# The last batch's gated expert product: weighing, transposed copies, output product and store divided over engines and halves

## The chip, the cores and the metric

The kernel runs on one core of a Trainium2 chip (trn2). The metric is the device time of one execution in microseconds (us), as the median of several runs.

## The reference, cut to what matters

A text stream `x` of 4 batches of 512 tokens by 128 channels goes through four residual blocks: a cross attention with a state-space filter, a butterfly feed-forward, a second cross attention, and a mixture of 8 experts of rank 32, of which each token takes the best two. Only the last block is touched:

```python
logits = jnp.einsum('bnd,de->bne', x, gate_w)      # x: after a layer norm
topv, topi = jax.lax.top_k(logits, 2)
w = jax.nn.softmax(topv, axis=-1)
u = jnp.einsum('bnd,edr->bner', x, Wu)
v = jnp.einsum('bnd,edr->bner', x, Wv)
s = jax.nn.silu(u) * v
Y = jnp.einsum('bner,erd->bned', s, Wo)
y_sel = jnp.take_along_axis(Y, topi[..., None], axis=2)
out = jnp.einsum('bnkd,bnk->bnd', y_sel, w)
# and around it
x = x + jnp.tanh(g_ffn[1]) * out
```

The kernel forms `s` for all 8 experts (8 times 32 = 256 columns), weighs it by the gate (zero for the experts that were not chosen), and multiplies by the 256 by 128 matrix `Wo`, which is the same sum.

## The kernel before, in words

Each batch's 512 tokens lie as four tiles (t = 0 to 3) of 128 tokens, one token per partition. The work is cut into steps with a name and a batch, such as `moe_out/3`; one table, `ORDER`, writes out by hand the order of the steps on each of the four compute engines: TensorE (PE), ScalarE (ACT), VectorE (DVE) and GpSimd (POOL). An engine takes its steps strictly in that order; a step waits on semaphores for what other engines have to have done. A second table, `BANKS`, gives the PSUM bank of each product; a product that reuses a bank first waits for the readers of the bank's former content. The four batches run interleaved, so while one batch waits on one engine the other engines have steps of other batches. Batch 3 is the last, and at its end there is nothing left to interleave.

The last block of one batch b is made of these steps:

- `top2` on DVE (with one exponential on ACT) makes the gate weights `W8`, 8 numbers for each token (L1305 to L1334).
- `units0` to `units3`: PE multiplies a token tile by `Wu` and `Wv`, 512 columns into one bank; ACT writes the silu of the first 256 columns to SBUF as tile t of `SUT` (L1000 to L1005); DVE multiplies it by the other 256 columns and counts up the semaphore `gated` (L1335 to L1338).
- `gate0` and `gate1` on POOL: each weighs two tiles of `SUT` (512 elements in each partition) by `W8`, and counts up `weighted` (L1573 to L1578).
- `turn0` and `turn1`: PE waits for both gate steps, and for each half j of the 256 columns transposes the four token tiles into a bank (L679 to L684, the transposes on L683). ACT copies each bank into `SU` (L1006 to L1010, through its helper on L837).
- `moe_out`: PE waits for both copies and makes the output product, 4 tiles by 2 halves j, 8 matmuls that the trace shows as 16 records (L685 to L692, through the helper on L499). DVE then adds the whole bank to `X` (L1339 to L1341, through the helper on L1118).
- SyncE (SP) waits for that addition and issues one store of the batch (L480 to L482), 256 KB, with 1 KB for each partition and half c of the tokens. At the very end it waits until all four stores have landed (L483).

The ends of the engines' orders before the change are: PE `units3/3 moe_out/2 turn0/3 turn1/3 moe_out/3`; ACT `units3/3 turn0/3 turn1/3`; DVE `units3/3 moe_out/2 moe_out/3`; POOL `gate0/3 gate1/3`.

In the trace, `SUT` lies in the buffer shown as `pack_bfly`, `SU` in `arena`, `W8` in `bt`, and all PSUM banks are shown as `bank`. POOL's element-wise helper is on L1496, ACT's on L837.

Of the kernel before, what the change touches and what calls it, by code (L numbers as in the profile page):

```python
# [7 lines left out]
B, S, D = 4, 512, 128  # L8
P = 128
NT = S // P  # L10
# [26 lines left out]
def columns(parts):  # L37
    at, out = 0, {}
    for name, n in parts:
# [46 lines left out]
        units1/1 units2/1 units3/1 lift4/3 wo/2 q/3 lift5/2 turn0/1 scoreA0/3 turn1/1 scoreA1/3 units0/2  # L86
        scoreA2/3 units1/2 scoreA3/3 units2/2 units3/2 maxT/3 keyA0/3 logits/2 keyA1/3 mixA0/3 keyA2/3 normA/3
        mixA1/3 mixA2/3 moe_out/1 wo/3 turn0/2 lift5/3 turn1/2 logits/3 units0/3 units1/3 units2/3 units3/3
        moe_out/2 turn0/3 turn1/3 moe_out/3
    """,  # L90
    "act": """
        s_kgen0 s_plag s_masks s_m0 s_qlag s_trig s_psin0 s_qsin rs0/0 score0/0 s_vw s_pexp winv0/0 score1/0
# [11 lines left out]
        rs3/3 rs5/1 keyA2/2 lift3/3 fold_up0/3 fold_up1/3 top2/1 rs4/3 normA/2 units0/1 units1/1 units2/1  # L104
        units3/1 lift4/3 q/3 lift5/2 turn0/1 rs5/2 turn1/1 units0/2 units1/2 units2/2 units3/2 maxT/3 keyA0/3
        keyA1/3 keyA2/3 top2/2 normA/3 turn0/2 lift5/3 turn1/2 rs5/3 top2/3 units0/3 units1/3 units2/3
        units3/3 turn0/3 turn1/3
    """,
    "dve": """
        s_kgen0 s_wq s_k0 s_consts s_coef s_parg0 s_parg1 s_qarg stat0/0 round0_0/0 round1_0/0 round2_0/0  # L110
# [17 lines left out]
        wo/1 norm2/3 stat5/1 x1/3 moe_out/0 stat3/3 norm3/3 top2/1 fold_down/3 stat4/3 normA/2 units0/1  # L128
        units1/1 units2/1 units3/1 wo/2 stat5/2 scoreA0/3 scoreA1/3 scoreA2/3 scoreA3/3 maxT/3 units0/2
        units1/2 units2/2 units3/2 top2/2 normA/3 wo/3 stat5/3 moe_out/1 top2/3 units0/3 units1/3 units2/3  # L130
        units3/3 moe_out/2 moe_out/3
    """,
    "pool": """
        s_row s_coef pick0/0 s_qal s_film pick1/0 s_ufly0 s_rows weigh0/0 s_ufly1 s_dfly0 s_dfly1 pick2/0
# [3 lines left out]
        gain/0 x1/0 mixi/1 s_v1 film_pre/1 k1/0 weigh1/2 weigh2/2 pick3/2 pick0/3 k1/1 weigh3/2 x_bias/1  # L138
        pick1/3 gain/1 x1/1 mixi/2 weigh0/3 mixr/2 film_pre/2 k1/2 weigh1/3 pick2/3 pick3/3 weigh2/3 weigh3/3
        x_bias/2 x_bias/3 gain/2 film_pre/3 mixi/3 gate0/0 gate1/0 gain/3 norm4/3 k1/3 gate0/1 gate1/1 gate0/2  # L140
        gate1/2 gate0/3 gate1/3
    """,
}

# [27 lines left out]
    "logits": [("logits", "logits")],  # L172
    **{f"units{t}": [(f"uv{t}", f"units{t}")] for t in range(NT)},
    **{f"turn{j}": [(f"turn{j}", f"turn{j}")] for j in range(2)},
    "moe_out": [("moe", "moe_out")],
    "s_k0": [("k0", "s_k0")], "s_m0": [(f"m0_{i}", "s_m0") for i in range(B)],
    "s_vw": [("wvf", "s_vw")], "vw": [("vw", "vw")],
    "s_w1": [("w1c", "s_w1")], "s_moe": [("moec", "s_moe"), ("goc", "s_moe")], "s_cw1": [("w1x", "s_cw1")], "s_cwup": [("wupx", "s_cwup")],
# [10 lines left out]
    for step, _, b, banks in ((*word.partition(":")[0].partition("/"), word.partition(":")[2]) for word in """  # L189
# [17 lines left out]
        scoreA1/3:4765 units0/2:1 scoreA2/3:7046 units1/2:2 scoreA3/3:0754 units2/2:0 units3/2:5 maxT/3:6  # L207
        keyA0/3:4607 logits/2:3 keyA1/3:4536 mixA0/3:72 keyA2/3:5140 moe_out/1:1 wo/3:0 turn0/2:7 lift5/3:6
        turn1/2:0 logits/3:4 units0/3:1 units1/3:6 units2/3:7 units3/3:5 moe_out/2:0 turn0/3:6 turn1/3:1
        moe_out/3:5  # L210
    """.split())
}

# [18 lines left out]
def build(nc, dram, out_dram):  # L232
# [5 lines left out]
    with ctx:  # L238
# [158 lines left out]
        def readers(name, b):  # L397
            if name.startswith("lift"):
                return [(lifted[int(name[4:])], b + 1)]
            if name.startswith("turn"):  # L400
                return [(s["turned"], 2 * b + int(name[4:]) + 1)]
            if name.startswith("uv"):
                return [(s["gated"], NT * b + int(name[2:]) + 1)]
            if name.startswith("score"):
                g = NT * b + int(name[5:])
                return [(s["first_round"], 2 * H0 * (g + 1)), (s["exps_done"], g + 1)]
            if name.startswith("sA"):
                g = NT * b + int(name[2])
                return [(s["maxed"], RG * g + int(name[4]) + 1)]
            if name.startswith("kA"):  # L410
                return [(s["probs_ready"], RG * (NCH * b + int(name[2])) + int(name[4]) + 1)]
            if name.startswith("up"):
                return [(s["up_gelu"], HT * b + int(name[2]) + 1)]
            if name.startswith("fup"):
                return [(s["fup_gelu"], HT * b + int(name[3]) + 1)]
            if name.startswith("kern"):
                return [(s["kern_copied"], int(name[4:]) + 1), (s["kern_moved"], int(name[4:]) + 1)]
            if name.startswith("m0_"):
                return [(s["m0_copied"], int(name[3:]) + 1)]
            if name.startswith("t1_"):  # L420
                return [(s["t1_copied"], 2)]
            return {
                "attnT": [(s["attnT_copied"], b + 1)], "fa": [(s["filmed"], b + 1)], "fb": [(s["filmed"], b + 1)],
                "down": [(x_ready["v"], b + 1)], "d0": [(s["dft_moved"], b + 1)],
                "d1": [(s["dft_copied"], 2 * b + 2)], "y": [(s["y_scaled"], b + 1)],
                "fc": [(s["ao_ready"], 2 * b + 1)], "fd": [(s["ao_ready"], 2 * b + 2)],
                "fdown": [(x_ready["x2"], b + 1)], "q": [(s["q_copied"], b + 1)],
                "mT": [(s["maxT_copied"], b + 1)], "pv": [(s["out_ready"], b + 1)], "sums": [(s["out_ready"], b + 1)],
                "wo": [(x_ready["x3"], b + 1)],
                "logits": [(s["logits_copied"], b + 1)],  # L430
                "moe": [(s["x4_ready"], b + 1)], "k0": [(s["k0_masked"], B)],
                "wvf": [(s["wvf_copied"], 1)], "moec": [(s["moe_centered"], 1)], "goc": [(s["moe_centered"], 3)], "w1x": [(s["w1_centered"], 1)], "wupx": [(s["wup_copied"], 2)], "vw": [(s["vw_copied"], b + 1)],
                "w1c": [(s["b1_done"], 1)], "fr0": [(s["freq_copied"], 2)], "fr1": [(s["freq_copied"], 3)],
                "wup": [(s["wup_copied"], 1)], "bup": [(s["bup_done"], 1)], "t2": [(s["t2_copied"], 1)],
                "wdn": [(s["wdn_copied"], 1)], "k1": [(s["k1_copied"], b + 1)],
                "v1a": [(s["v1_masked"], B - 1)], "v1b": [(s["v1_masked"], B)],
            }[name]
# [19 lines left out]
        def _(sp):  # L457
# [19 lines left out]
                sp.dma_start(by_parity(X[:, b, :, :]), tokens(dram["x"][b])).then_inc(x_loaded[b], 16)  # L477
            for name in ("rows", "att1", "moe"):
                sp.dma_start(packs[name][0][:, :], dram[name]).then_inc(loaded[name], 16)
            for b in range(B):  # L480
                sp.wait_ge(s["x4_ready"], b + 1)
                sp.dma_start(tokens(out_dram[b]), by_parity(X[:, b, :, :])).then_inc(stored, 16)  # L482
            sp.wait_ge(stored, 16 * B)  # L483


        @block.tensor
        def _(pe):
            I = part("first", "I")

            def claim(name, b):  # L490

                former = BEFORE[name, b]
                if former is not None:
                    for semaphore, value in readers(*former):
                        pe.wait_ge(semaphore, value)
                return bank(name, b)
# [14 lines left out]
            for step, b in SCHEDULE["pe"]:  # L511
# [160 lines left out]
                elif step.startswith("units"):  # L672
                    pe.wait_ge(lifted[5], b + 1)
                    if b == 0:
                        pe.wait_ge(s["moe_centered"], 2)
                    a, z = MOE["wu"][0], MOE["wv"][1]
                    mm(claim(f"uv{tile}", b)[:, :], LO[:, b, P * tile:P * tile + P], packs["moe"][0][:, a:z])\
                        .then_inc(s["u_ready"], 1)
                elif step.startswith("turn"):  # L679
                    pe.wait_ge(s["weighted"], 2 * b + 2)  # L680
                    o = claim(step, b)
                    for t in range(NT):
                        last = nc.tensor.transpose(o[:, P * t:P * t + P], SUT[:, t, P * tile:P * tile + P], I)  # L683
                    last.then_inc(s["turn_ready"], 1)  # L684
                elif step == "moe_out":  # L685
                    o = claim("moe", b)
                    pe.wait_ge(s["turned"], 2 * b + 2)
                    for t in range(NT):
                        for j in range(2):
                            last = mm(o[:, P * t:P * t + P], SU[:, j, P * t:P * t + P], wom[:, j, :],  # L690
                                      start=j == 0, stop=j == 1)
# [422 lines left out]
        def _(dve):  # L1114
# [26 lines left out]
            for step, b in SCHEDULE["dve"]:  # L1141
# [193 lines left out]
                elif step.startswith("units"):  # L1335
                    dve.wait_ge(s["silu_ready"], NT * b + tile + 1)
                    x = SUT[:, tile, :]
                    tt(x, bank(f"uv{tile}", b)[:, NE * RE:2 * NE * RE], x, ALU.mult).then_inc(s["gated"], 1)  # L1338
                elif step == "moe_out":  # L1339
                    dve.wait_ge(s["moe_ready"], 2 + b + 1)  # L1340
                    tt(flat(X[:, b, :, :]), bank("moe", b)[:, :], flat(X[:, b, :, :]), ALU.add).then_inc(s["x4_ready"], 1)  # L1341
# [141 lines left out]
        def _(pool):  # L1483
# [53 lines left out]
            for step, b in SCHEDULE["pool"]:  # L1537
# [30 lines left out]
                elif step == "gain":  # L1568
                    pool.wait_ge(*normed(2, b))
                    pool.wait_ge(s["rows_ready"], 1)  # L1570
                    tt(XG[:, b, :, :], XG[:, b, :, :], part("rows", "gno").unsqueeze(1).broadcast_to([P, NT, D]), ALU.mult)\
                        .then_inc(s["gained"], 1)
                elif step.startswith("gate"):  # L1573
                    pool.wait_ge(s["gated"], NT * b + 2 * tile + 2)
                    pool.wait_ge(s["gate_ready"], b + 1)
# [292 lines left out]
```

## Time and profile before

| what | value |
|---|---|
| median of 3 runs | 334.61 us (334.46 to 335.09) |
| the profiled execution's own time | 336.93 us |
| its span, first to last instruction | 335.1 us |
| granted TensorE clock, mean over the span | 0.903 |
| busy share PE, DVE, ACT, POOL | 77%, 78%, 67%, 56% |
| instructions | 6215 |
| DMA moved | 10.28 MB |

All rows below come from one profiled execution. A row of a timeline has a start (us from the span's start), a length (us; for several instructions of a kind from the first's start to the last's end), engine, line, operation, output and inputs, and count; in brackets is how long the engine sat idle before it and what ended that. Instructions of one engine overlap a little, so x4 in 1.54 us can be four of 0.42 us. "PEld" is TensorE's weight load; "SPq" is a DMA issue on SP.

### The profile page before, as it was taken

Reading aid. Unit: us, or ns where it says so; the run is one execution under the profiler, and the core shown is the slowest. Engines: PE = TensorE matmul, PEld = TensorE weight load, DVE = VectorE, ACT = ScalarE, POOL = GpSimd, SP = SyncE. Lnnn points to the kernel's source line nnn. Section 1 sums busy time; section 2 is a strip of 40 time slices with the busy share of each in tenths; the row PEclk is TensorE's granted clock in tenths of the full one; section 3 lists DMA queues with packets and bytes.
Section 4 is the critical chain, followed back from the end, with each engine's and each line's share of the span. In section 5 each row is a group of like instructions: output and inputs, shape, how many; then the busy total and the mean of one; then the engine's idle time right before and its main releaser. Section 6 shows DMA issues by size and latency. Waiting matters only on the chain.

```text
span 335.1 us, 6215 instructions
## 1 busy us (share of the span) xinstructions
PE 258.3 (77%) x1778; PEld 162.7 (49%) x1778; DVE 261.9 (78%) x1354; ACT 226.1 (67%) x534; POOL 188.6 (56%) x268
## 2 busy tenths in 40 slices
PE   1810008087588588899999989999999999989994
PEld 0510005066346258657686543865535837534463
DVE  3999999999997998998999876599537853674171
ACT  4899996740823674588877957957767477668461
POOL 2379999689999959765769777457002010600211
PEclk9975556789677779799999999999999999999999
DMA  7990000000000000000000000000000000000001
GB/s 244 398 388 28 1 1 4 1 1 3 0 0 1 0 4 0 0 4 0 2 1 0 3 0 3 0 3 1 2 0 0 2 31 4 0 0 2 2 31 63
DMA packets 4663, 10.28 MB, mean 31 GB/s; under 512 B 659, under 2 KB 2836, under 8 KB 4374
## 3 DMA queue, kind: packets, MB, share of 16 engines
q1 hardware_dynamic: 4630, 9.89, 8.0%
q8 instruction: 14, 0.23, 0.3%
q14 instruction: 19, 0.16, 0.2%
HBM read 8.84 MB, written 1.05 MB: 30 GB/s over the span
## 4 chain that ended last, share of the span: by engine, by line
PE 47%; DVE 17%; POOL 15%; ACT 10%; issue 6%; POOLq 0%; ACTq 0%; DVEq 0%
PE bank L499 43%; ACT arena L837 5%; POOL arena L1496 5%; POOL MT L1496 4%; DVE arena L1118 4%; DVE R L1216 3%; DVE V L1204 2%; PE bank L521 2%; POOL k0bd L1496 1%; DVE KT L1447 1%; POOL bt L1496 1%; POOL sel L1606 1%; PE bank L683 1%; ACT E L837 1%; DVE st L1150 1%
## 5 line engine op out<-in xcount | busy, mean ns | idle before, releaser
L837 ACT ACTIVATE arena<-bank 128x512 f32<-128x512 f32 (+2 forms) x63 | 32.8, 597 | 21.2 <-PE bank L499 14.3
L1216 DVE MATCH_REPLACE8 R<-V,R 128x77 f32<-128x77 f32 x192 | 40.6, 223 | 0.0
L831 ACT ACT_TABLE_LOAD x29 | 37.2, 1283 | 4.2 <-DMA pack_kgen<-in_kgen 3.7
L1496 POOL TENSOR_TENSOR pack_bfly<-pack_bfly,bt 128x512 f32<-128x512 f32 x8 | 8.2, 1048 | 52.4 <-DVE bt L1118 42.7
L499 PE MATMUL bank<-arena 128*32 128x16 f32 (+3 forms) x304 | 13.2, 223 | 30.9 <-DVE arena L1118 29.6
L1204 DVE MAX8 V<-R 128x8 f32<-128x77 f32 x192 | 31.1, 224 | 0.4
L1174 DVE TENSOR_REDUCE bt<-bank 128x4 f32<-128x308 f32 x64 | 25.8, 468 | 5.8 <-PE bank L499 5.7
L499 PEld LDWEIGHTS bank<-arena 128*32 128x32 f32 (+1 forms) x304 | 9.9, 143 | 36.4 <-DVE arena L1118 31.2
L837 ACT ACTIVATE E<-bank,negm,rs 128x77 f32<-128x77 f32 x64 | 21.3, 415 | 7.3 <-POOL sel L1496 5.3
L499 PE MATMUL bank<-pack_bfly,arena 32*128 32x512 f32 (+3 forms) x136 | 21.0, 528 | 1.0 <-ACT pack_bfly L837 0.7
L1496 POOL TENSOR_TENSOR k0bd<-sel,w 128x308 f32<-128x308 f32 x16 | 11.6, 727 | 15.3 <-ACT w L837 15.0
L499 PE MATMUL bank<-pack_moe,LO 128*128 128x512 f32 (+1 forms) x64 | 19.6, 432 | 0.8 <-DVE bt L1174 0.5
L499 PE MATMUL bank<-LO,pack_ffn 128*128 128x512 f32 x32 | 17.8, 706 | 0.7 <-ACT LO L837 0.7
L499 PE MATMUL bank<-VW,AT 78*128 78x128 f32 x128 | 16.1, 279 | 2.4 <-ACT pack_dft L837 0.9
L1606 POOL TENSOR_SCALAR sel<-R 128x308 f32<-128x308 f32 x16 | 16.0, 1001 | 3.2 <-issue 2.2
L837 ACT ACTIVATE arena<-MT 128x128 f32<-128x128 f32 x74 | 17.3, 428 | 0.5 <-DVE MT L1118 0.5
L499 PEld LDWEIGHTS bank<-VW,AT 78*128 78x128 f32 x128 | 15.0, 192 | 4.3 <-ACT AT L837 2.0
L499 PE MATMUL bank<-arena,pack_dft 128*128 128x256 f32 x48 | 14.5, 447 | 2.5 <-DVE arena L1118 2.5
L1496 POOL TENSOR_TENSOR XG<-XG,pack_rows 128x512 f32<-128x512 f32 x4 | 5.1, 1272 | 18.9 <-DVE XG L1123 18.9
L499 PEld LDWEIGHTS bank<-pack_dft,arena 128*128 128x128 f32 x128 | 14.9, 192 | 1.1 <-issue 1.0
L1216 DVE MATCH_VALUE_LOAD R<-V,R 128x8 f32 x192 | 15.2, 79 | 0.4 <-POOL sel L1496 0.4
L499 PEld LDWEIGHTS bank<-pack_ffn,arena 128*128 128x128 f32 x128 | 14.9, 192 | 0.8 <-ACT arena L837 0.7
(232 smaller groups left out, 754.6 us busy)
## 6 DMA issues: line engine op xcount, KB each, us to landing
pack_bfly<-in_bfly SPq DMA_DIRECT2D x1, 2420.0 KB, 9.9
LO<-in_xT SPq DMA_DIRECT2D x4, 256.0 KB, 10.8
X<-in_x SPq DMA_DIRECT2D x4, 256.0 KB, 11.2
pack_dft<-in_dft SPq DMA_DIRECT2D x1, 1024.0 KB, 12.1
out_x<-X SPq DMA_DIRECT2D x4, 256.0 KB, 2.1
pack_ffn<-in_ffn SPq DMA_DIRECT2D x1, 512.0 KB, 12.6
pack_moe<-in_moe SPq DMA_DIRECT2D x1, 452.0 KB, 9.6
pack_film<-in_film SPq DMA_DIRECT2D x1, 432.0 KB, 4.5
```

Source lines behind the costliest of these rows:

```text
L499: return nc.tensor.matmul(out, lhsT, rhs, start=start, stop=stop, **kw)
L521: last = nc.tensor.transpose(o[:, P * t:P * t + P], src[:, b, t, :], I)
L683: last = nc.tensor.transpose(o[:, P * t:P * t + P], SUT[:, t, P * tile:P * tile + P], I)
L831: nc.scalar.add_instruction(mybir.InstLoadActFuncSet(name=nc.get_next_instruction_name(), act_func_set_id=need, ins=[], outs=[]))
L837: return nc.scalar.activation(out, in_, func, **kw)
L1118: return nc.vector.tensor_tensor(out, x, y, op)
L1150: linked(nc.vector.bn_stats(st6[:, n, t, :], src[:, b, t, :]))
L1174: nc.vector.tensor_reduce(mx1[:, b % 2, tile, r, :], bank(f"sA{tile}_{r}", b)[:, 0:FLAT] .rearrange("p (h k) -> p h k", h=HG), AX.X, ALU.max)\
L1204: top = nc.vector.max(V8[:, g % 2, h, r, :], src[h])
L1216: swap = nc.vector.match_replace(R8[:, g % 2, r % 2, h, :], V8[:, g % 2, h, r, :], src[h], NEG)
L1496: return nc.gpsimd.tensor_tensor(out, x, y, op)
L1606: chain(nc.gpsimd.tensor_scalar(sel[:, g % 2, :, :], R8[:, g % 2, 1, :, :], -1.0e38, None, ALU.is_le))
```

## The change

For batches 0 to 2 nothing changes. For batch 3:

- **Gate.** POOL's `gate0/3` weighs tiles 0 and 1 in two instructions of 256 elements, each waiting only for its own tile, and counts up `weighted` once after both. `gate1/3` moves to DVE, right behind `units3/3`: one instruction over tiles 2 and 3.
- **Transposes.** PE transposes tiles 0 and 1 of both halves j as soon as POOL's part is done, then, after DVE's part, tiles 2 and 3 of both halves.
- **Copies.** ACT copies half 0 (`turn0/3`); DVE copies half 1 (`turn1/3`).
- **Output.** `moe_out/3` makes token tiles 0 and 1 only, `moe_rest/3` tiles 2 and 3, into a bank of its own. DVE adds each half by itself, and SP issues one store of 128 KB for each.
- On DVE, `moe_out/2` (the addition of batch 2) now stands behind `gate1/3` and `turn1/3`.

```diff
 "pe":    ... moe_out/2 turn0/3 turn1/3 moe_out/3
+          moe_rest/3
 "act":   ... units3/3 turn0/3
-         turn1/3
 "dve":   ... units3/3
+         gate1/3 turn1/3
          moe_out/2 moe_out/3
+         moe_rest/3
 "pool":  ... gate0/3
-         gate1/3
...
+"moe_rest": [("moe_rest", "moe_rest")]      # PSUM_USE; BANKS gains moe_rest/3:7
...
-            for b in range(B):
+            for b in range(B - 1):
                 sp.wait_ge(s["x4_ready"], b + 1)
                 sp.dma_start(tokens(out_dram[b]), by_parity(X[:, b, :, :])).then_inc(stored, 16)
-            sp.wait_ge(stored, 16 * B)
+            for c in range(2):
+                sp.wait_ge(s["x4_ready"], B + c)
+                sp.dma_start(tokens(out_dram[B - 1])[:, c], by_parity(X[:, B - 1, :, :])[:, c]).then_inc(stored, 16)
+            sp.wait_ge(stored, 16 * (B + 1))
...
+                elif step.startswith("turn") and b == B - 1:
+                    if tile == 0:
+                        pe.wait_ge(s["weighted"], 2 * b + 1)
+                        claim("turn0", b)
+                        claim("turn1", b)
+                    else:
+                        pe.wait_ge(s["gated"], NT * B + 1)
+                    for j in range(2):
+                        for t in (2 * tile, 2 * tile + 1):
+                            last = nc.tensor.transpose(bank(f"turn{j}", b)[:, P * t:P * t + P], SUT[:, t, P * j:P * j + P], I)
+                        if tile == 1:
+                            last.then_inc(s["turn_ready"], 1)
...
-                elif step == "moe_out":
-                    o = claim("moe", b)
+                elif step in ("moe_out", "moe_rest"):
+                    o = claim("moe" if step == "moe_out" else "moe_rest", b)
                     pe.wait_ge(s["turned"], 2 * b + 2)
-                    for t in range(NT):
+                    for t in (range(NT) if b < B - 1 else range(0, 2) if step == "moe_out" else range(2, NT)):
...
+                elif step == "gate1":
+                    dve.wait_ge(s["gated"], NT * b + NT)
+                    dve.wait_ge(s["gate_ready"], b + 1)
+                    x = SUT[:, 2:4, :].rearrange("p t (e r) -> p t e r", e=NE)
+                    tt(x, x, W8[:, b % 2, 2:4, :].unsqueeze(3).broadcast_to([P, 2, NE, RE]), ALU.mult).then_inc(s["gated"], 1)
+                elif step == "turn1":
+                    dve.wait_ge(s["turn_ready"], 2 * b + 2)
+                    dve.wait_ge(s["moe_ready"], 2 + b)
+                    nc.vector.tensor_copy(SU[:, 1, :], bank("turn1", b)[:, :]).then_inc(s["turned"], 1)
+                elif step in ("moe_out", "moe_rest") and b == B - 1:
+                    half = int(step == "moe_rest")
+                    dve.wait_ge(s["moe_ready"], 2 + b + 1 + half)
+                    x, part2 = X[:, b, 2 * half:2 * half + 2, :], slice(256 * half, 256 * half + 256)
+                    tt(flat(x), bank("moe_rest" if half else "moe", b)[:, part2], flat(x), ALU.add).then_inc(s["x4_ready"], 1)
...
+                elif step.startswith("gate") and b == B - 1:
+                    pool.wait_ge(s["gate_ready"], b + 1)
+                    for i in range(2):
+                        pool.wait_ge(s["gated"], NT * b + i + 1)
+                        x = SUT[:, i, :].rearrange("p (e r) -> p e r", e=NE)
+                        last = tt(x, x, W8[:, b % 2, i, :].unsqueeze(2).broadcast_to([P, NE, RE]), ALU.mult)
+                    last.then_inc(s["weighted"], 1)
```

## Rows read from the trace of the kernel before

**Rows 1.** Timeline of the last stretch, all engines, from 324 us to the end.

```profile
324.89 1.54 DVE L1118 TENSOR_TENSOR pack_bfly<-bank,pack_bfly 128x256 f32<-128x256 f32 x4 [0.40 <-ACT pack_bfly L837]
325.24 1.95 PE L499 MATMUL bank<-pack_moe,arena 128*128 128x128 f32 x16
325.76 2.05 POOL L1496 TENSOR_TENSOR pack_bfly<-pack_bfly,bt 128x512 f32<-128x512 f32 x2 [8.98 <-DVE pack_bfly L1118]
327.23 0.69 DVE L1118 TENSOR_TENSOR X<-bank,X 128x512 f32<-128x512 f32 x1 [0.80 <-PE bank L499]
327.87 1.09 PE L683 MATMUL bank<-pack_first,pack_bfly 128*128 128x128 f32 x8 [0.68 <-POOL pack_bfly L1496]
328.56 1.08 ACT L837 ACTIVATE arena<-bank 128x512 f32<-128x512 f32 x2 [2.59 <-PE bank L683]
329.79 2.02 PE L499 MATMUL bank<-pack_moe,arena 128*128 128x128 f32 x16 [0.83 <-ACT arena L837]
331.85 0.69 DVE L1118 TENSOR_TENSOR X<-bank,X 128x512 f32<-128x512 f32 x1 [3.93 <-PE bank L499]
...
332.57 0.37 SPq L482 DMA_DIRECT2D out_x<-X  x1
```

**Rows 2.** Chain of waits over the same stretch: start, us, what.

```profile
326.81 1.02 POOLq L238
...
329.00 0.65 ACTq L238
329.65 0.14 issue
```

**Rows 3.** Timeline of short stretches, where single instructions stand apart.

```profile
324.89 0.42 DVE L1118 TENSOR_TENSOR pack_bfly<-bank,pack_bfly 128x256 f32<-128x256 f32 x1 [0.40 <-ACT pack_bfly L837]
...
325.76 1.05 POOL L1496 TENSOR_TENSOR pack_bfly<-pack_bfly,bt 128x512 f32<-128x512 f32 x1 [8.98 <-DVE pack_bfly L1118]
...
329.05 0.59 ACT L837 ACTIVATE arena<-bank 128x512 f32<-128x512 f32 x1
```

**Rows 4.** Busy time by stretch after the last store's issue.

```profile
core 0: us, PE busy (x) PEld busy (x) DVE busy (x) ACT busy (x) POOL busy (x), PEclk, DMA share, GB/s
333.40:333.60 0.20, 0.00 (x0) 0.00 (x0) 0.00 (x0) 0.00 (x0) 0.00 (x0) 1.00 0.52 189
...
334.20:334.40 0.20, 0.00 (x0) 0.00 (x0) 0.00 (x0) 0.00 (x0) 0.00 (x0) 1.00 0.26 82
```

**Rows 5.** POOL's groups by shape: line, form, count, busy us, mean ns, idle before.

```profile
L1496 POOL TENSOR_TENSOR arena<-v,pack_bfly 128x512 f32<-128x512 f32 x4 | 4.1, 1047 | 0.1
...
L1496 POOL TENSOR_TENSOR arena<-v,pack_bfly 128x128 f32<-128x128 f32 x4 | 1.5, 400 | 0.1
```

**Rows 6.** DVE's groups by shape, same columns.

```profile
L1174 DVE TENSOR_REDUCE bt<-bank 128x4 f32<-128x308 f32 x64 | 25.8, 468 | 5.8 <-PE bank L499 5.7
...
L1118 DVE TENSOR_TENSOR XG<-HN,XG 128x512 f32<-128x512 f32 x4 | 2.8, 690 | 0.1
...
L1122 DVE TENSOR_SCALAR arena<-arena 128x1152 f32<-128x1152 f32 x1 | 0.8, 760 | 0.2 <-ACT arena L837 0.2
```

**Rows 7.** Timeline, DVE and POOL, short stretches at 232 and 233 us.

```profile
232.13 0.73 POOL L1496 TENSOR_TENSOR arena<-arena 128x256 f32<-128x256 f32 x1
...
232.19 1.23 DVE L1118 TENSOR_TENSOR MT<-arena,pack_film 128x512 f32<-128x512 f32 x1
...
233.34 0.68 DVE L1118 TENSOR_TENSOR MT<-arena,pack_film 128x512 f32<-128x512 f32 x1
```

**Rows 8.** POOL's instructions on one tile: form, ns min/median/max, first and last start.

```profile
L1496 POOL TENSOR_TENSOR k0bd<-sel,w x16: 696/699/1146, 42.7 to 211.6; 128x308 f32<-128x308 f32 x16
```

**Rows 9.** The four stores of L482: time from issue to landing.

```profile
DMA to landing us min/median/max: 2.1/2.1/2.2
```

**Rows 10.** Timeline of SP at the start, and the page's DMA issues (KB, us to landing).

```profile
0.73 0.39 SPq L458 DMA_DIRECT2D pack_kgen<-in_kgen  x1
1.18 0.42 SPq L459 DMA_DIRECT2D pack_small<-in_small  x1
...
pack_kgen<-in_kgen SPq DMA_DIRECT2D x1, 320.0 KB, 2.9
pack_small<-in_small SPq DMA_DIRECT2D x1, 14.5 KB, 2.6
```

More of the change, by code:

```diff
@@ L88 @@
         mixA1/3 mixA2/3 moe_out/1 wo/3 turn0/2 lift5/3 turn1/2 logits/3 units0/3 units1/3 units2/3 units3/3
-        moe_out/2 turn0/3 turn1/3 moe_out/3
+        moe_out/2 turn0/3 turn1/3 moe_out/3 moe_rest/3
     """,
@@ L106 @@
         keyA1/3 keyA2/3 top2/2 normA/3 turn0/2 lift5/3 turn1/2 rs5/3 top2/3 units0/3 units1/3 units2/3
-        units3/3 turn0/3 turn1/3
+        units3/3 turn0/3
     """,
@@ L130 @@
         units1/2 units2/2 units3/2 top2/2 normA/3 wo/3 stat5/3 moe_out/1 top2/3 units0/3 units1/3 units2/3
-        units3/3 moe_out/2 moe_out/3
+        units3/3 gate1/3 turn1/3 moe_out/2 moe_out/3 moe_rest/3
     """,
@@ L140 @@
         x_bias/2 x_bias/3 gain/2 film_pre/3 mixi/3 gate0/0 gate1/0 gain/3 norm4/3 k1/3 gate0/1 gate1/1 gate0/2
-        gate1/2 gate0/3 gate1/3
+        gate1/2 gate0/3
     """,
@@ L174 @@
     **{f"turn{j}": [(f"turn{j}", f"turn{j}")] for j in range(2)},
-    "moe_out": [("moe", "moe_out")],
+    "moe_out": [("moe", "moe_out")], "moe_rest": [("moe_rest", "moe_rest")],
     "s_k0": [("k0", "s_k0")], "s_m0": [(f"m0_{i}", "s_m0") for i in range(B)],
@@ L209 @@
         turn1/2:0 logits/3:4 units0/3:1 units1/3:6 units2/3:7 units3/3:5 moe_out/2:0 turn0/3:6 turn1/3:1
-        moe_out/3:5
+        moe_out/3:5 moe_rest/3:7
     """.split())
@@ L430, in readers @@
                 "logits": [(s["logits_copied"], b + 1)],
-                "moe": [(s["x4_ready"], b + 1)], "k0": [(s["k0_masked"], B)],
+                "moe": [(s["x4_ready"], b + 1)], "moe_rest": [(s["x4_ready"], B + 1)], "k0": [(s["k0_masked"], B)],
                 "wvf": [(s["wvf_copied"], 1)], "moec": [(s["moe_centered"], 1)], "goc": [(s["moe_centered"], 3)], "w1x": [(s["w1_centered"], 1)], "wupx": [(s["wup_copied"], 2)], "vw": [(s["vw_copied"], b + 1)],
```

## The prediction

> **What bounds the kernel now.** I read the chain of waits first, then the timeline of the last 12 us, because the change touches nothing earlier: every table entry for batches 0 to 2 and for batch 3 up to `units3/3` stands as it was. In that stretch no engine is full. It is a relay: DVE gates four tiles, POOL weighs them in two pieces, PE transposes, ACT copies twice, PE makes the product, DVE adds, SP stores [rows 1]. The chain shows two places where a second piece of work queues behind a first on the same engine: POOL's second weighing (1.02 us) and ACT's second copy (0.65 us, then 0.14 us until PE starts) [rows 2]. PE sits idle for 0.68 us before the transposes and for 0.83 us before the product, DVE for 3.93 us before the last addition [rows 1]. So DVE has room exactly where POOL and ACT are late. Behind the last addition (331.85 + 0.69 = 332.54) come the store's issue at 332.57 [rows 1], a silent time, the transfer itself and a tail to the span's end at 335.10. The transfer is half on in the slice from 333.40 and a quarter on in the one from 334.20 [rows 4], so data moves from about 333.50 to 334.25: 0.75 us for 256 KB. From issue to first data is 0.93 us, from last data to the end 0.85 us.
>
> **The change part by part.** A time after "at" is on the clock of the profiled execution.
>
> *Gate on POOL.* The four gating multiplies start at 324.89, each 0.42 us long [rows 3], 1.54 us in all [rows 1], so one every (1.54 - 0.42)/3 = 0.37 us; they end at 325.31, 325.68, 326.06 and 326.43. POOL started 0.08 us after the second end, at 325.76. It now starts after the first: 325.39. A weighing of 256 elements is not in the trace; between 400 ns for 128 and 1047 ns for 512 elements [rows 5], both with a repeated operand as here, a straight line gives 0.62 us (bounds 0.53, half of 1.05 [rows 3], and 0.73, the 256-element form of [rows 7]). Its two pieces end at about 326.0 and 326.6.
>
> *Gate on DVE.* It can start at 326.43 + 0.03 = 326.46. Two SBUF inputs of 512 elements take 0.69 us [rows 6]: end at 327.15. Here is the one place where engines can get in each other's way. At 232 us, a DVE instruction of this kind began while POOL was at work and took 1.23 us; the same form took 0.68 us right after, when POOL was done [rows 7]. POOL had 0.67 us left when DVE began and DVE lost 0.55. In the new order POOL has about 0.15 us left when DVE begins, so I add 0.13: end at 327.28. The Trainium skill says the same as a rule (GPSIMD Engine Reference, Key points): the two engines share SBUF interfaces and contend when a DVE instruction has two SBUF inputs. It speaks against this change, and the rows bear it out; taken as full exclusion it is a rival below.
>
> *PE, transposes.* PE's own work is the limit here: `moe_out/2` runs until 325.24 + 1.95 = 327.19, its last matmul starting 0.27 earlier. Eight transposes take 1.09 us [rows 1]; with the last one also 0.27 long they start every 0.117 us. The first four can start at about 327.04, as POOL was done at 326.6, and the fifth at 327.51, while DVE's part is ready from 327.28 + 0.06 = 327.34. So all eight run back to back: the sixth, which completes half 0, ends at 327.90, the eighth at 328.13. Before they ended at 328.96. The waits added on PE hold up nothing.
>
> *Copies.* ACT copies half 0 from 327.92 to 328.51 (0.59 [rows 3]). DVE copies half 1 from 328.15. No such copy out of PSUM by DVE is in the trace. Lower bound 0.42 us: 1152 elements of SBUF, one input, in 0.76 us [rows 6], scaled with 0.16 fixed. Upper bound 0.69, the 512-element addition out of PSUM [rows 1]. Nearest is the reduction that reads 308 elements of PSUM in 0.468 us [rows 6]; at the 1.05 ns per element between 256 and 512 (0.42 and 0.69) this makes 0.68. I take 0.69: end at 328.84. The Trainium skill (VectorE: DVE Perf Modes, "Why PSUM operands drop a tier") holds that any fp32 PSUM operand keeps DVE at its basic rate. No trace here shows it for a copy; by the SBUF rate the end would be 0.27 us earlier, though then PE would wait for DVE at 328.57.
>
> *Output product.* Before, POOL's end to PE's start took 0.06 us, ACT's end (329.64) to PE's start 0.15 [rows 1]. I take 0.06 (0.15 is kept for the range): PE starts at 328.90 instead of 329.79. That is the first gain, 0.89 us. Sixteen records in 2.02 us, the last 0.28 long, come every 0.116 us, so the first eight end at 328.90 + 1.09 = 329.99 and the last at 330.92.
>
> *Additions.* The first half runs from 330.01 to 330.43, under the product. The second, 0.42 instead of 0.69, starts at 330.94 and ends at 331.36: a further 0.27 us off the path, and 332.54 - 331.36 = 1.18 us in sum. The displaced `moe_out/2` on DVE starts at 328.84 instead of 327.23 and ends at 329.53, before the first half needs DVE at 330.01. It costs nothing; if PE were 0.5 us faster it would.
>
> *Stores.* SP issues batch 2's store at 329.56, the halves at 330.46 and 331.39. An issue takes 0.37 us, so none waits for SP. With 0.93 us to first data, batch 2 moves from 330.49 to 331.24, the first half from 331.39 to 331.77, the second from 332.32 for half of 0.75, that is 0.375 us: to 332.70. Then the 0.85 us tail: end at 333.55 against 335.10. The bounds for this last saving are 0 and 0.375 us.
>
> **Sum.** 0.89 (product starts earlier) + 0.27 + 0.02 (addition; rounding of handovers) + 0.375 (store) = 1.55 us. The profiled execution took 336.93 us, with 1.83 us outside its span, and would take 335.38. The median of the runs is 334.61, which is 2.32 less; I carry the difference over: 333.06.
>
> **Rivals.**
> 1. *Half a store costs as much as a whole one.* Landing is 2.1 to 2.2 us for all four stores [rows 9], all of one size, so the trace does not show how it scales; but 0.75 us of it is visibly data. For it: what is silent may hide a fixed part. Then only 1.18 is gained: 333.43.
> 2. *DVE and POOL shut each other out.* POOL too is slowed: a form of 0.70 us took 1.15 once [rows 8]. If POOL's second piece stretches by that ratio it ends at 326.99, and DVE, waiting it out (+0.53), ends at 327.68. The fifth transpose then starts at 327.74, not 327.51: 0.23 us lost, 333.3. This is the skill's rule at full strength, and only the short overlap speaks against it.
> 3. *Little is left.* Handovers at 0.15 instead of 0.06 at the new DVE steps, rivals 1 and 2 together, and a repeated operand that slows DVE's weighing: 1.55 - 0.375 - 0.23 - 0.3 = 0.65 us: 334.0.
> 4. *Slower: the stores line up.* Batch 2's store is moved by 1.6 us, next to two others on one queue. If a store only begins when the former has landed, at 2.1 us each they land at 331.66, 333.76 and 335.86, and with the 0.43 us between landing (332.57 + 2.1) and the end the span is 336.3: 1.2 us slower, 335.8. It decides from 1.92 us per store upwards (then the end is 0.67 us later than before). Against it: at the start SP issues 0.45 us apart and the second load has landed by 3.8 us, 0.15 after the first at 3.6 [rows 10], so queued transfers overlap.
>
> **How the numbers follow.** A measurement of this kernel tells some 0.2% (0.67 us) from no change. Forecast 0.62 (own range 332.7 to 333.4); rival 1 0.15, rival 2 0.10, rival 3 0.09, rival 4 0.04. The first three are faster by more than 0.2% (0.87), rival 3 is within it, rival 4 is slower (0.04). The range 332.5 to 334.0 goes from the forecast with a fast DVE copy (0.27 less) and a run at the low end of the spread of before, up to rival 3.
>
> **What would show it.** Right: PE's transposes start near 327.0 with no gap inside, ACT and DVE copies overlap, the product starts about 0.9 us earlier, two 256-element additions of 0.42 us, three stores issued near 329.6, 330.5 and 331.4, and data of the last one for 0.4 us. Wrong: a DVE weighing over 0.95 us or a gap among the eight transposes (rival 2), a landing of the last store above 2.0 us (rival 1), transfers that follow each other only after landing (rival 4), or a product that starts later than 329.3.

## The result

The changed kernel took 333.72 us (median of 19 runs, 332.83 to 339.79), the kernel before 335.34 us (19 runs, 334.46 to 341.30), measured side by side. The ratio is 0.9957, with a 95% interval of 0.9941 to 0.9974: 1.4 us less, 0.9 to 2.0 by the interval. The forecast was a ratio of 0.9954 (333.06 against 334.61). Six of these 38 executions, and two of the twelve in the second timing further down, took 339.8 to 341.3 us, whichever the kernel; the medians count them, the ratios leave them out.

The interval holds the forecast, but also rival 1 (1.18 us less), so the run time alone does not tell which mechanism was right. The two profiled executions differ by much more: spans of 335.1 and 331.1 us. The page of the changed kernel:

```profile
span 331.1 us, 6218 instructions
...
PE 256.6 (77%) x1778; PEld 162.3 (49%) x1778; DVE 262.4 (79%) x1357; ACT 225.4 (68%) x533; POOL 188.0 (57%) x268
...
PEclk9965557679797789999999999999999999999999
```

Three instructions more on DVE, one less on ACT. The clock row has low digits only in its first half. Where the 4.0 us went is seen from the last stretch of the same timeline as [rows 1] (rows of PE's weight loads are left out, here and below):

```profile
322.47 1.54 DVE L1134 TENSOR_TENSOR pack_bfly<-bank,pack_bfly 128x256 f32<-128x256 f32 x4 [0.40 <-ACT pack_bfly L853]
322.82 1.95 PE L502 MATMUL bank<-pack_moe,arena 128*128 128x128 f32 x16
323.04 1.19 POOL L1527 TENSOR_TENSOR pack_bfly<-pack_bfly,bt 128x256 f32<-128x256 f32 x2 [8.68 <-DVE pack_bfly L1134]
324.04 0.74 DVE L1134 TENSOR_TENSOR pack_bfly<-pack_bfly,bt 128x512 f32<-128x512 f32 x1
...
324.61 1.04 PE L692 MATMUL bank<-pack_first,pack_bfly 128*128 128x128 f32 x8
325.46 0.60 ACT L853 ACTIVATE arena<-bank 128x512 f32<-128x512 f32 x1 [1.92 <-PE bank L692]
325.68 0.69 DVE L1364 COPY arena<-bank 128x512 f32<-128x512 f32 x1 [0.91 <-PE bank L692]
326.29 0.68 DVE L1134 TENSOR_TENSOR X<-bank,X 128x512 f32<-128x512 f32 x1
...
326.52 2.02 PE L502 MATMUL bank<-pack_moe,arena 128*128 128x128 f32 x16 [0.88 <-DVE arena L1364]
327.69 0.42 DVE L1134 TENSOR_TENSOR X<-bank,X 128x256 f32<-128x256 f32 x1 [0.71 <-PE bank L502]
328.14 1.24 SPq L485 DMA_DIRECT2D out_x<-X  x2
328.58 0.42 DVE L1134 TENSOR_TENSOR X<-bank,X 128x256 f32<-128x256 f32 x1 [0.47 <-PE bank L502]
```

The first gating multiply of batch 3, with nothing changed ahead of it, already starts 2.42 us earlier (322.47, before 324.89). That is no effect of the change, as shown below. I therefore measure everything by the **tail**, from the start of that multiply to the end of the span. The page rounds the span to a tenth; the trace ends at 335.103 and 331.133 us. So the tail is 335.10 - 324.89 = 10.21 us before and 331.13 - 322.47 = 8.67 us now (from unrounded times), a gain of 1.55 us. The forecast was 1.55. The expectations below still reckon with the rounded span, that is with a tail of 8.63 us; tails given as measured are unrounded throughout. In every profiled execution the granted clock is 1.00 (the upper level, 2.4 GHz) in the whole tail.

Matched instruction by instruction, DVE in the changed kernel's execution is 0.7 us ahead from 12 us on, which is while the first loads come in, and 2.4 us ahead from 139 us on; the step in between falls after 124 us. Busy time by stretch in the two kernels, 120 to 140 us, first before, then changed:

```profile
120.00:140.00 20.00, 17.42 (x109) 14.39 (x107) 17.51 (x88) 10.38 (x27) 13.45 (x20) 0.90 0.01 1
```

```profile
120.00:140.00 20.00, 16.57 (x121) 14.61 (x122) 19.26 (x104) 11.37 (x33) 15.51 (x21) 1.00 0.01 2
```

The kernel before was granted 0.90 there, the changed one 1.00 throughout, and got more instructions done on every engine. The clock is not the whole of it: in the ten profiled executions with 1.00 in this stretch the tail began anywhere from 322.37 to 323.71 us, in the two with 0.90 and 0.91 at 324.89 and 324.07, and in the two with 0.83 at 329.29 and 329.73. Whether the clock moves the start, or both follow from something else, was not tried.

That the change has no part in it is seen from the spans of the second timing, of the executions that the ratio counts: 332.6 to 334.8 us for the kernel before and 331.1 to 333.2 us for the changed one. Less a tail of 10.21 and 8.67 us, both kernels reach the tail between 322.4 and 324.6 us: an estimate, since only the profiled executions show the tail itself.

### The profile page after: what moved, and what is told of

It is laid out like the page before. It is cut to its first block, busy times and chain, and to the rows that moved or that the text cites. A ratio compares the mean times of both kernels' runs of the same rounds, so it can differ in the third digit from the quotient of the medians.

```text
span 331.1 us, 6218 instructions
## 1 busy us (share of the span) xinstructions
PE 256.6 (77%) x1778; PEld 162.3 (49%) x1778; DVE 262.4 (79%) x1357; ACT 225.4 (68%) x533; POOL 188.0 (57%) x268
## 3 DMA queue, kind: packets, MB, share of 16 engines
HBM read 8.84 MB, written 1.05 MB: 30 GB/s over the span
## 4 chain that ended last, share of the span: by engine, by line
PE 45%; POOL 18%; DVE 16%; ACT 11%; issue 6%; POOLq 0%; DVEq 0%
PE bank L502 41%; ACT arena L853 5%; POOL arena L1527 5%; POOL MT L1527 4%; DVE R L1232 3%; DVE arena L1134 3%; DVE V L1220 2%; PE bank L524 2%; POOL k0bd L1527 2%; POOL sel L1645 1%; POOL sel L1527 1%; DVE KT L1478 1%; ACT L847 1%; POOL XG L1527 1%; POOL bt L1527 1%
## 5 line engine op out<-in xcount | busy, mean ns | idle before, releaser
L1527 POOL TENSOR_TENSOR pack_bfly<-pack_bfly,bt 128x512 f32<-128x512 f32 (+1 forms) x8 | 7.3, 939 | 52.1 <-DVE bt L1134 42.7
L502 PE MATMUL bank<-arena 128*32 128x16 f32 (+3 forms) x304 | 11.8, 218 | 28.6 <-DVE arena L1134 26.8
L502 PE MATMUL bank<-LO,pack_ffn 128*128 128x512 f32 x32 | 16.5, 663 | 0.7 <-ACT LO L853 0.7
L502 PE MATMUL bank<-M,LO 128*128 128x308 f32 x32 | 12.7, 486 | 4.0 <-ACT E L853 3.1
```

The costliest lines, as they stand in the source:

```text
L502: return nc.tensor.matmul(out, lhsT, rhs, start=start, stop=stop, **kw)
L1527: return nc.gpsimd.tensor_tensor(out, x, y, op)
```

## The experiments

Each experiment is read by its tail. Each edit is against the changed kernel, unless it says otherwise.

**One store instead of two.**

```diff
-            for c in range(2):
-                sp.wait_ge(s["x4_ready"], B + c)
-                sp.dma_start(tokens(out_dram[B - 1])[:, c], ...)
+                sp.wait_ge(s["x4_ready"], B + 1)
+                sp.dma_start(tokens(out_dram[B - 1]), by_parity(X[:, B - 1, :, :]))
```

> The changed kernel with one change undone: the last batch goes out in one store of 256 KB, issued after the second half's addition. I measure by the tail: from the start of batch 3's first gating multiply on DVE to the end of the span; it was 10.21 us in the kernel before (324.89 to 335.10) and 8.63 us in the changed one (322.47 to 331.10), in which the stretch from the last store's issue to the end fell from 2.53 to 2.06 us. Theory (the transfer time of the second 128 KB is what was saved, with a little more behind it): the tail is 9.10 us, issue to end 2.5 us. Rival (a store costs the same whatever its size, and the 0.47 us came from elsewhere, such as the emptier queue): the tail stays at 8.6 us and issue to end at 2.1 us.

Measured: tail 9.10 us (from 323.64 to 332.74). The last store's row in the timeline:

```profile
330.20 0.37 SPq L482 DMA_DIRECT2D out_x<-X  x1
```

From there to the end are 2.54 us, against 331.13 - 329.03 = 2.10 in the changed kernel. So a half store is cheaper by 0.43 us. The landing says the same: 2.14 us after the issue for 256 KB, 1.71 us for 128 KB. Rival 1 falls.

**Product, addition and store whole.**

```diff
-        moe_out/2 turn0/3 turn1/3 moe_out/3 moe_rest/3
+        moe_out/2 turn0/3 turn1/3 moe_out/3
```

(DVE and SP accordingly: one addition, one store.)

> The changed kernel with output product, addition and store of the last batch whole again; gate and copies stay shared. Theory (the parts add up): the product still ends 6.07 us after the first gating multiply, the addition takes 0.69 instead of 0.42 us and the store 2.53 instead of 2.06 us, so the tail is 8.63 + 0.27 + 0.47 = 9.37 us, and the front part (first gating multiply to the product's start, 4.05 us) does not change. Rival (the halves also make the product itself or its start later, by a second bank and a second wait): the product's start moves below 4.0 us or its 2.02 us shrinks, and the tail is under 9.2 us.

Measured: tail 9.37 us; the product starts at 4.05 and ends at 6.08. Exactly the addition's 0.27 and the store's 0.43 us are lost, nothing in front moves.

**Both copies on ACT.**

```diff
-        units3/3 turn0/3                    # act
+        units3/3 turn0/3 turn1/3
-        units3/3 gate1/3 turn1/3 moe_out/2  # dve
+        units3/3 gate1/3 moe_out/2
```

> The changed kernel with both transposed copies on ACT again; everything else stays. Theory (with the gate shared, the copies are limited by the eighth transpose and not much by ACT): ACT's second copy starts about 0.49 us after the first and ends 0.17 us later than DVE's does now, so the tail is 8.80 us: sharing the copies is worth under 0.2 us by itself. Rival (the copies were the main bottleneck, as the 0.65 us in the chain of the kernel before suggests): the tail is over 9.1 us.

Measured: tail 8.84 us, 0.17 more. ACT's second copy ends 0.17 us later than DVE's did and the product starts at 4.22 instead of 4.05; that is all of it. The rival falls.

**POOL weighs all four tiles.**

```diff
-        gate1/2 gate0/3                     # pool
+        gate1/2 gate0/3 gate1/3
-        units3/3 gate1/3 turn1/3 moe_out/2  # dve
+        units3/3 turn1/3 moe_out/2
-                        pe.wait_ge(s["gated"], NT * B + 1)
+                        pe.wait_ge(s["weighted"], 2 * b + 2)
```

> The changed kernel with all four tiles weighed by POOL, one instruction each, and PE's second group of transposes waiting for POOL; copies, product and stores stay shared and halved. Theory: POOL's pieces start every 0.57 us, the fourth ends 2.9 us after the first gating multiply (DVE's weighing ended at 2.31), the fifth transpose starts 0.35 to 0.40 us later than now, and the tail is 9.0 us. Rival (DVE's weighing disturbed POOL, so that POOL alone is quicker than its parts say): the fourth piece ends by 2.6 us and the tail is under 8.8 us.

Measured: tail 9.10 us, 0.43 more. The timeline of POOL and PE there:

```profile
324.64 2.34 POOL L1527 TENSOR_TENSOR pack_bfly<-pack_bfly,bt 128x256 f32<-128x256 f32 x4 [8.68 <-DVE pack_bfly L1134]
...
326.21 0.60 PE L692 MATMUL bank<-pack_first,pack_bfly 128*128 128x128 f32 x4
327.03 0.66 PE L692 MATMUL bank<-pack_first,pack_bfly 128*128 128x128 f32 x4 [0.22 <-POOL pack_bfly L1527]
```

PE waits 0.22 us between its two groups of transposes, and the product starts at 4.49 instead of 4.05. POOL's pieces come every 0.57 us with or without DVE's weighing beside them, and the fourth ends 2.91 us after the first gating multiply: the theory.

**POOL weighs its two tiles in one instruction.**

```diff
-                    for i in range(2):
-                        pool.wait_ge(s["gated"], NT * b + i + 1)
-                        ...                               # 256 elements each
+                    pool.wait_ge(s["gated"], NT * b + 2)
+                    ...                                   # 512 elements
```

> The changed kernel with POOL weighing tiles 0 and 1 in one instruction of 512 elements that waits for both, as before; DVE still weighs tiles 2 and 3. POOL then starts 0.87 us after the first gating multiply and DVE 1.57 us after it, so they overlap for some 0.35 us instead of 0.19. Theory (they share access and DVE loses nearly the overlap): DVE's weighing takes 0.9 to 1.05 us instead of 0.74, POOL's at least its 1.05 us; PE's first four transposes still start at 2.14 because of its own earlier work, the fifth about at 2.65, and the tail is 8.65 to 8.8 us. Rival (no contention when one operand is the short repeated one): DVE's takes 0.74 us or less and the tail stays 8.63 us. In either case POOL's split into two instructions is worth under 0.2 us.

Measured: tail 8.73 us, 0.06 more. Timeline of the two weighings:

```profile
324.44 1.05 POOL L1527 TENSOR_TENSOR pack_bfly<-pack_bfly,bt 128x512 f32<-128x512 f32 x1 [9.03 <-DVE pack_bfly L1134]
...
325.07 0.96 DVE L1134 TENSOR_TENSOR pack_bfly<-pack_bfly,bt 128x512 f32<-128x512 f32 x1
```

DVE's weighing takes 0.96 us while POOL is still at work for 325.49 - 325.07 = 0.42 us. In the changed kernel POOL had 324.23 - 324.04 = 0.19 us left and DVE took 0.74; in the next experiment POOL was done and it took 0.68. POOL's own 1.05 us is not stretched. So the rival falls: the two engines contend with this repeated operand too. PE's earlier work hides most of it: the transposes end 0.07 us later.

**DVE's addition of batch 2 in its old place.**

```diff
-        units3/3 gate1/3 turn1/3 moe_out/2
+        units3/3 moe_out/2 gate1/3 turn1/3
```

> The changed kernel with DVE's addition of batch 2 in its old place, directly behind the four gating multiplies and ahead of the weighing. Theory: it waits there for PE's product of batch 2 (2.30 us after the first gating multiply), runs 0.69 us, and pushes the weighing to 3.05 us: the fifth transpose starts at 3.8 instead of 2.6 us and the tail is 9.8 us, which eats three quarters of the gain. Rival (the order on DVE does not matter much, since DVE is idle most of the time): the tail is under 9.0 us.

Measured: tail 9.83 us, 1.16 more. DVE and PE there:

```profile
332.06 0.69 DVE L1134 TENSOR_TENSOR X<-bank,X 128x512 f32<-128x512 f32 x1 [0.80 <-PE bank L502]
332.67 0.68 DVE L1134 TENSOR_TENSOR pack_bfly<-pack_bfly,bt 128x512 f32<-128x512 f32 x1
...
333.41 0.66 PE L692 MATMUL bank<-pack_first,pack_bfly 128*128 128x128 f32 x4 [0.95 <-DVE pack_bfly L1134]
```

DVE waits 0.80 us for PE, then adds, and only then weighs; PE's second group waits 0.95 us for that. Without the least visible line of the change, the displaced addition, only 0.39 of the 1.55 us would be left.

**The shared copy alone, on the kernel before.**

```diff
-        units3/3 turn0/3 turn1/3            # act
+        units3/3 turn0/3
-        units3/3 moe_out/2 moe_out/3        # dve
+        units3/3 moe_out/2 turn1/3 moe_out/3
```

> The kernel before with one part of the change alone: DVE copies the second transposed half, behind its addition of batch 2; gate, transposes by half, product, addition and store as before. The tail before was 10.21 us. Theory: alone the shared copy is worth nothing, because the second half's transposes end 0.42 us after the first's, and DVE's copy of 0.69 us from there ends within 0.05 us of ACT's, which ran 0.49 us behind its first: tail 10.2 us. Rival (the 0.65 us for which the chain has the second copy queued on ACT is what sharing removes): tail 9.6 to 9.9 us.

Measured: tail 10.26 us, 0.05 more than before. In its timeline the copies run side by side:

```profile
332.96 0.60 ACT L837 ACTIVATE arena<-bank 128x512 f32<-128x512 f32 x1 [2.59 <-PE bank L683]
...
333.39 0.69 DVE L1342 COPY arena<-bank 128x512 f32<-128x512 f32 x1 [1.08 <-PE bank L683]
...
334.23 2.02 PE L499 MATMUL bank<-pack_moe,arena 128*128 128x128 f32 x16 [0.88 <-DVE arena L1342]
```

DVE waited for the second half's transposes: its copy starts 0.44 us after ACT's, while in the kernel before ACT started its own second copy 0.49 us after its first. And DVE needs 0.69 us where ACT needs 0.59. So DVE's copy ends 0.04 us later than ACT's second one did. The 0.65 us that the chain put on ACT's queue [rows 2] was not there to be removed.

**Weighing and transposes alone.** Both copies on ACT, product, addition and store whole (the second and third edits above together).

> The changed kernel with only the shared weighing and the transposes by token halves left; both copies on ACT, product, addition and store whole. Theory (the parts add): tail 9.36 us of the kernel with a whole product, plus the 0.22 us that the copies on ACT cost, is 9.58 us, so this part is worth 0.63 us of the 1.58. Rival (the sharing of the weighing and of the copies only work together): tail 9.9 us or more.

Measured: tail 9.54 us. The parts thus stand as a staircase:

| kernel | tail, us | step |
|---|---|---|
| before | 10.21 | |
| weighing shared, transposes by token halves | 9.54 | 0.68 |
| copies shared as well | 9.37 | 0.17 |
| product and addition halved as well | 9.10 | 0.26 |
| store halved as well (the changed kernel) | 8.67 | 0.43 |

(Steps from unrounded tails.) The first step bundles four things: DVE's share of the weighing, POOL's two smaller instructions, the displaced addition, and the transposes by token halves. Undone one at a time in the changed kernel, the first costs 0.43, the second 0.06 and the third 1.16 us; these overlap and do not add up. The transposes by token halves were never undone by themselves. Nor do the steps hold in another order: the shared copies are worth 0.17 us here, but nothing when they come first.

**A step beyond: copies by token halves.** Tiles 0 and 1 are transposed into two banks of their own, so that their copies (256 elements each) and the first half of the product do not wait for tiles 2 and 3.

```diff
-        moe_out/2 turn0/3 turn1/3 moe_out/3 moe_rest/3    # BANKS turn0/3:6 turn1/3:1
+        moe_out/2 flip0/3 flip1/3 moe_out/3 moe_rest/3    # BANKS flip0/3:61 flip1/3:23
+                elif step.startswith("flip"):             # on DVE; ACT's is the same with half 0
+                    dve.wait_ge(s["turn_ready"], 2 * b + 2 * tile + 2)
+                    dve.wait_ge(s["moe_ready"], 2 + b)
+                    nc.vector.tensor_copy(SU[:, 1, 256 * tile:256 * tile + 256], bank(f"flip{tile}1", b)[:, 0:256])
```

> A step beyond the changed kernel: the transposes of token tiles 0 and 1 go to two banks of their own and are copied (256 elements each by ACT and DVE) while tiles 2 and 3 are still being transposed; the product of the first half of the tokens waits only for those. Theory: first copies end 3.2 us after the first gating multiply, the product starts at 3.35 instead of 4.05, nothing behind it changes, and the tail is 7.92 us. Rival (the second half's copies, which wait for DVE's weighing, then set the end, or four smaller copies cost as much as two): the product has a gap between its halves and the tail is 8.2 us or more.

Measured: tail 7.96 us, 0.71 less than the changed kernel. Its timeline:

```profile
324.51 1.04 PE L693 MATMUL bank<-pack_first,pack_bfly 128*128 128x128 f32 x8
324.93 0.82 ACT L857 ACTIVATE arena<-bank 128x256 f32<-128x256 f32 x2 [1.48 <-PE bank L693]
325.15 0.86 DVE L1372 COPY arena<-bank 128x256 f32<-128x256 f32 x2 [0.48 <-PE bank L693]
325.72 2.02 PE L505 MATMUL bank<-pack_moe,arena 128*128 128x128 f32 x16 [0.17 <-DVE arena L1372]
```

PE idles 0.17 us before the product instead of 0.88, and the product has no gap: 2.02 us again.

**Timed together: the changed kernel, the step beyond, and one with a third part.** The third part splits the last half of product, addition and store into tile 2 and tile 3:

```diff
+            for j in range(2):
+                sp.wait_ge(s["x4_ready"], B + 1 + j)
+                sp.dma_start(tokens(out_dram[B - 1])[:, 1, j], X[:, B - 1, 2 + j, :])
```

> The changed kernel as it is, timed beside the kernel before and the two below. All theories: tail 8.63 us again within 0.03, whatever the span does ahead of it; ratio to the kernel before about 0.9953 (1.58 of 334.6 us), with a scatter of the stretch ahead of the tail of some 2 us from execution to execution that the tail does not share.

> The kernel with the copies by halves of the tokens, timed (one look at it gave a tail of 7.93 us). Theory: tail 7.93 us, 2.28 us less than before, ratio 0.9932. Rival (the time is lost elsewhere in most executions): ratio no lower than the changed kernel's.

> The same with the last half of product, addition and store cut once more: tiles 2 and 3 each have a product in a bank of its own, an addition of 128 elements, and a store of 64 KB in runs of 512 B. Theory (every size term shrinks in proportion): the last addition takes 0.29 instead of 0.42 us, the last transfer about 0.19 instead of 0.38 us, so the tail is 7.6 us. Rival (the store's time goes by its number of runs, which stays 128, or a third store behind the second waits on the queue): the last issue to end stays at 2.05 us or rises, and the tail is 7.8 us or more.

| kernel | tail, us | median, us (runs) | ratio to before, 95% interval |
|---|---|---|---|
| before | 10.21 | 335.42 (17) | |
| changed | 8.67 | 333.94 (12) | 0.9950 (0.9931 to 0.9970) |
| copies by token halves | 7.97 | 333.26 (6) | 0.9940 (0.9917 to 0.9963) |
| three parts as well | 7.88 | 332.69 (6) | 0.9931 (0.9906 to 0.9957) |

The changed kernel's tail is the same as the first time within 0.01 us, and so is that of the copies by halves (7.97 and 7.96). The order of the medians is that of the tails, but the intervals overlap: that the two further kernels beat the changed one is shown by their tails and not by their run times.

The third part brought 0.09 us where 0.3 was expected. Its last issue, and the busy stretches of its last transfer:

```profile
328.70 0.44 SPq L490 DMA_DIRECT2D out_x<-X  x1
```

```profile
329.60:329.80 0.20, 0.00 (x0) 0.00 (x0) 0.00 (x0) 0.00 (x0) 0.00 (x0) 1.00 0.62 192
329.80:330.00 0.20, 0.00 (x0) 0.00 (x0) 0.00 (x0) 0.00 (x0) 0.00 (x0) 1.00 0.48 136
```

The same for the last 128 KB of the changed kernel, issued at 329.03:

```profile
329.80:330.00 0.20, 0.00 (x0) 0.00 (x0) 0.00 (x0) 0.00 (x0) 0.00 (x0) 1.00 0.46 169
330.00:330.20 0.20, 0.00 (x0) 0.00 (x0) 0.00 (x0) 0.00 (x0) 0.00 (x0) 1.00 1.00 358
330.20:330.40 0.20, 0.00 (x0) 0.00 (x0) 0.00 (x0) 0.00 (x0) 0.00 (x0) 1.00 0.39 128
```

The shorter addition did gain its 0.13 us, but SP lost them again: the addition ends at 328.54, while the issue before it runs from 328.20 to 328.66, so the last issue is 0.13 us late. The transfer shrank nearly as the theory said, to (0.62 + 0.48) x 0.20 = 0.22 us of busy time against 0.37. But an issue with runs of 512 B takes 0.44 us instead of 0.34, and the data begin 0.94 us after its start instead of 0.84. So from issue to end are 2.02 us, against 2.09 to 2.11 for the second half in all kernels with two halves: 0.08 us saved, and not 0.19. The tail is where the rival had put it (7.8 us or more), but neither of the rival's reasons is shown as it stands: the transfer did not stay the same, and what queued was the issue on SP, not the data.

## Why the prediction was right

The forecast's own steps, in us after the first gating multiply (324.89 before), beside the changed kernel:

| step | forecast | measured |
|---|---|---|
| POOL's first piece starts | 0.50 | 0.57 |
| DVE's weighing starts; takes | 1.57; 0.82 | 1.57; 0.74 |
| eight transposes start; take | 2.15; 1.09 | 2.14; 1.04 |
| ACT's copy starts | 3.03 | 3.00 |
| DVE's copy starts; takes | 3.26; 0.69 | 3.21; 0.69 |
| output product starts | 4.01 | 4.05 |
| second addition ends | 6.47 | 6.54 |
| last store issued | 6.50 | 6.57 |
| end | 8.66 | 8.67 |

The mechanism was right term by term: no step of the relay waited for anything but what the prediction named. That the sum is right to the hundredth is luck. Its terms were 0.89 us for the earlier product, 0.29 for the addition with the rounding, and 0.375 for the store; measured they are 0.85, 0.27 and 0.43. The first two were taken too large, the last too small, and the errors cancel.

- *POOL's piece of 256 elements*: 0.62 us taken from a straight line, 0.62 measured. It starts 0.14 instead of 0.08 us after the multiply that it waits for; nobody waits for that.
- *Contention of DVE and POOL*: 0.13 us was added, 0.06 was paid, although POOL had 0.19 us left and not 0.15. By the forecast's own row (0.67 left, 0.55 lost) the loss is some 0.13 us less than what is left, so 0.13 was too much. It was hidden, as the forecast said: the fifth transpose waited for nothing. Rival 2 had a mechanism that exists, but the overlap was too short for it to matter, and POOL's second piece was not stretched. That PE's earlier work covers it is shown by the one-instruction weighing, which cost DVE 0.28 us and the tail 0.06.
- *DVE's copy out of PSUM*: 0.69, the upper bound. The Trainium skill (VectorE: DVE Perf Modes, "Why PSUM operands drop a tier") says that an fp32 operand in PSUM keeps DVE at its basic rate. The trace now agrees: the copy of 512 elements took 0.69 us, as long as the addition out of PSUM. (The prediction's "no such copy" holds for this size only: the trace before has 32x64 copies out of PSUM on DVE, 0.27 to 0.28 us each, too short to read the rate from.)
- *Handover from copy to product*: the term that was furthest off. 0.06 was taken, 0.14 to 0.15 measured in every kernel of this study, whichever engine copied last and however long the copy. The forecast had read the 0.15 and kept it for the range only. The product still started only 0.04 us later than forecast, because the copies started 0.05 us earlier. Transposes behind POOL or DVE start after 0.05 to 0.06. Why the product's handover is longer was not tried.
- *Displaced addition of batch 2*: free, as forecast, and moving it back costs 1.16 us.
- *Stores*: the second half's data moved for 0.37 us (forecast 0.375); the silent times around it were together 0.05 us shorter than taken (1.73 against 1.78). The second half was issued at 329.03, before the first, issued at 328.14 and landing after 1.7 us, was down, and its landing took no longer for that (1.71 us). So a store does not wait until the one before it has landed, and rival 4 is out.
- *Median*: 1.4 us and, in the second timing, 1.7 us (335.42 times 0.0050) against 1.55. Both intervals hold it, and the first (0.9 to 2.0 us less) leaves out the 0.65 us of rival 3. In absolute terms the forecast, 333.06 us, is 0.66 us below the 333.72 measured: within the stated range up to 334.0, but outside the forecast's own narrower range up to 333.4. The change is not at fault. The forecast started from a median of three executions of the kernel before, 334.61 us, and with 19 that median is 335.34.

The forecast did not say how the 0.89 us of an earlier product start divide between weighing and copies. The runs do: the product starts 0.68 us earlier by the first step of the staircase and 0.17 by the second, 0.85 in all. The copies' part only exists because the transposes now complete the halves 0.22 us apart and not 0.44.

## What to carry to other kernels

At the end of a kernel, where nothing is left to interleave, work it out as a relay: every share or split is worth only what its successor was really waiting for, and a queue time in the chain is no measure of it (0.65 us shown, nothing gained by the copy alone). Look as well at what else stands in the queue of the engine that takes the work over: here its place in DVE's order decided over 1.16 of 1.55 us. When single executions scatter by more than the change is worth, compare a stretch that begins at a fixed instruction; here it repeated within 0.01 us while the whole scattered by over 2. Take both of its ends unrounded: with the page's span, rounded to a tenth, the same two tails seemed to differ by 0.06 us.

## What the runs showed of the hardware

- A DVE instruction with two SBUF inputs that starts while POOL works is longer by nearly the time that POOL still needs: 0.19 us left cost 0.06, 0.42 left cost 0.28, and 0.67 left cost 0.55 [rows 7]; in all three the loss is what was left less 0.12 to 0.14 us. POOL's instruction, which had begun first, kept its length (1.05 us).
- It went the other way as well, in one case where POOL began second. In the kernel before, POOL's form of 0.70 us took 1.15 us the one time [rows 8] that it began while such a DVE instruction, started at 93.17, still had 0.58 us to go; the loss, 0.45 us, is again what was left less 0.13.

```profile
93.17 0.75 DVE L1118 TENSOR_TENSOR MT<-arena,pack_film 128x512 f32<-128x512 f32 x1
93.34 1.15 POOL L1496 TENSOR_TENSOR k0bd<-sel,w 128x308 f32<-128x308 f32 x1
```

- A store of 128 KB in 1 KB runs took 0.43 us less from issue to end than one of 256 KB (2.10 and 2.53); cutting it again, into 64 KB in runs of 512 B, gave 0.08 us more, since SP's issue grew from 0.34 to 0.44 us.
- PE's first matmul of the output product started 0.14 to 0.15 us after the last copy that it waits for, its first transpose behind POOL or DVE after 0.05 to 0.06. The cause is open.
- The start of the tail moved by 2.5 us between twelve executions whose instructions ahead of it are the same, and by 7.4 us with the other two. Those with a lower granted clock from 120 to 140 us came later, but at the same clock there it still moved by 1.3 us.
